# Graph attention over 8192 nodes on one core: the two dense inputs loaded as 128-row tiles, and row 0's store moved

## The reference

```python
h = jnp.maximum(_layernorm(x, axis=-1), 0.0)
g = inlayer2 @ W.T + b
f1 = g @ w1 + b1
f2 = g @ w2 + b2
logits = f1[:, None] + f2[None, :]
bias_mat = NEG_BIG * (1.0 - (adj > 0).astype(jnp.float32))
coefs = jax.nn.softmax(jax.nn.leaky_relu(logits, 0.01) + bias_mat, axis=-1)
out = x + coefs @ h
```

## Time and profile before

| What | Value |
|---|---|
| median of 3 runs | 1447.62 us (1447.36 to 1449.03) |
| the profiled execution's own time | 1447.61 us |
| its span, first to last instruction | 1445.8 us |
| PE busy | 1409.0 us (97%), 12623 matmuls |
| DVE busy | 1279.7 us (89%) |
| ACT busy | 612.7 us (42%) |
| POOL busy | 266.7 us (18%) |
| moved by DMA | 302.43 MB in 110184 packets |
| granted TensorE clock, mean | 0.990 |

### The profile page before, as it was taken

The page is one execution under the profiler, slowest core; times in us unless marked ns, Lnnn a source line. Parts: engine busy times, 40 slices in busy tenths (PEclk is TensorE's granted clock), DMA queues, the critical chain, the costliest instruction groups (busy, mean ns, idle before and its releaser), DMA issues.

```text
span 1445.8 us, 33385 instructions
## 1 busy us (share of the span) xinstructions
PE 1409.0 (97%) x12623; PEld 1246.9 (86%) x12623; DVE 1279.7 (89%) x1315; ACT 612.7 (42%) x713; POOL 266.7 (18%) x266
## 2 busy tenths in 40 slices
PE   8589899999999999999999999999999999999998
PEld 7468788888888888888888888888888888888887
DVE  5999898989989898998989899898998989899894
ACT  2895343444434344443434444343443434444330
POOL 0683111101101111110111111011111101111110
PEclk9799999999999999999999999999999999999999
DMA  9977999999999999999999999999999999999940
GB/s 293 316 177 167 228 233 235 234 235 221 209 210 215 209 210 210 214 210 208 216 207 211 211 213 211 208 216 206 213 213 211 210 209 215 209 209 216 208 108 14
DMA packets 110184, 302.43 MB, mean 209 GB/s; under 512 B 11732, under 2 KB 44628, under 8 KB 110164
## 3 DMA queue, kind: packets, MB, share of 16 engines
q1 hardware_dynamic: 100080, 289.52, 89.3%
q10 hardware_dynamic: 10084, 12.65, 3.0%
HBM read 293.73 MB, written 8.39 MB: 209 GB/s over the span
## 4 chain that ended last, share of the span: by engine, by line
PE 91%; DMA 4%; ACT 3%; issue 1%; DVE 1%; SPq 0%; ACTq 0%; POOL 0%; DVEq 0%; POOLq 0%
PE acc L1043 59%; PE acc L1045 29%; DMA adj_sb<-in_adj_dram 4%; PE rp L998 2%; ACT mask L561 1%; ACT h_f L577 1%; SPq L341 0%; ACT rp L561 0%; DMA w<-in_L_gnn_w_dram 0%; ACT H L583 0%; PE rp L1012 0%; PE small L985 0%; PE rp L1006 0%; DVE wgt L832 0%; ACTq L336 0%
## 5 line engine op out<-in xcount | busy, mean ns | idle before, releaser
L1043 PE MATMUL acc<-H,wT 128*128 128x257 f16 x8192 | 1356.7, 274 | 13.6 <-DVE wT L842 4.9
L1045 PE MATMUL acc<-H,wT 128*128 128x257 f16 x4096 | 1120.2, 273 | 0.0
L1043 PEld LDWEIGHTS acc<-H,wT 128*128 128x128 bf16 x8192 | 802.3, 98 | 116.4 <-issue 10.1
L561 ACT ACTIVATE mask<-adj_sb 128x1024 bf16<-128x1024 int32 x504 | 519.6, 1053 | 548.2 <-DVE wgt L832 432.8
L842 DVE STREAM_TRANSPOSE wT<-wgt 128x1024 f32<-128x1024 f32 x512 | 633.7, 1239 | 129.9 <-PE acc L1045 129.8
L832 DVE SCALAR_TENSOR_TENSOR wgt<-b_word,c_word,mask 128x1024 f32<-128x1024 f32 x504 | 628.7, 1260 | 3.6 <-ACT mask L561 3.6
L1045 PEld LDWEIGHTS acc<-H,wT 128*128 128x128 f16 x4096 | 401.9, 98 | 50.6
L481 POOL TENSOR_TENSOR x_res<-o_room,x_res 128x256 f32<-128x256 f32 x63 | 65.9, 1046 | 1100.6 <-ACT o_room L568 1077.4
L568 ACT ACTIVATE o_room<-acc,r_den 128x256 f32<-128x256 f32 x63 | 29.8, 474 | 230.6 <-DVE r_den L861 230.6
L486 POOL TENSOR_TENSOR o_room<-o_room,x_res 128x256 f32<-128x256 f32 x63 | 81.5, 1293 | 5.3
L483 POOL TENSOR_SCALAR o_room<-h_mean,no_nb 128x256 f32<-128x256 f32 x63 | 61.1, 969 | 0.0
(11 more groups left out here) (93 smaller groups left out, 163.4 us busy)
## 6 DMA issues: line engine op xcount, KB each, us to landing
adj_sb<-in_adj_dram SPq DMA_DIRECT2D x504, 512.0 KB, 8.5
x_res<-in_x_dram SPq DMA_DIRECT2D x64, 128.0 KB, 4.0
out_dram<-o_room SPq DMA_DIRECT2D x63, 128.0 KB, 4.3
H<-in_x_dram ACTq DMA_DIRECT2D x16, 256.0 KB, 12.7
H<-in_x_dram SPq DMA_DIRECT2D x16, 256.0 KB, 13.1
adj_sb<-in_adj_dram ACTq DMA_DIRECT2D x8, 512.0 KB, 14.3
wgt<-in_L_gnn_inlayer_dram ACTq DMA_DIRECT2D x8, 256.0 KB, 9.8
wgt<-in_L_gnn_inlayer_dram SPq DMA_DIRECT2D x8, 256.0 KB, 10.3
```

Of the source, the lines that this page charges most:

```text
L561: nc.scalar.activation(place, adj_sb[:, c, g * CQ:(g + 1) * CQ], ACT.Relu, scale=M_SCALE).then_inc(m_ready, 1)
L1043: pe.matmul(acc[:, par, 0:DV], w_hi[:, slot, t, :], H[:, j, part, 0:DV], start=(j == 0 and part == 0), stop=False)
L1045: mm = pe.matmul(acc[:, par, 0:DV], w_lo[:, slot, t, :], H[:, j, 0, 0:DV], start=False, stop=(j == ROWS - 1))
```

## The change

1. `load_strip` no longer loads a group of 32 partitions (8 rows of 1 KB for each) but a tile t of 128 rows over all partitions (1 KB each). A strip takes eight transfers of 128 KB in place of four of 256 KB, SP issues tiles 0 to 3 and ACT tiles 4 to 7. The bytes, the 1 KB pieces and the places where they land are the same. The waits for a strip count to 128 in place of 64. In memory the source of one transfer is four blocks, 1024 rows apart, of 32 adjacent rows; its outermost count is 4, where that of the destination is 128. Before, both outermost counts were 32.
2. SP stores row 0, and loads `x` for row 2, after it has issued the first chunk of row 4, not before (`store_row`, and one row more ahead of SP's loop).
3. Four small moves: ACT issues its half of row 1's first chunk before `values(2)`, not after its high half; ACT makes the first two mask parts of row 2 after the last high halves; DVE makes `weights(0, 0, 1)` ahead of `low_of_values(7)`; the mean of `h` is made one strip earlier on PE and two earlier on DVE.

```diff
-    x_q = x.rearrange("(c q k t s) d -> c k q s t d", c=NCH, q=Q, k=SC, t=TS)
-    in2_q = inlayer2.rearrange("(c q k t s) d -> c k q s t d", c=NCH, q=Q, k=SC, t=TS)
+    x_t = x.rearrange("(c q k t s) d -> c k t q s d", c=NCH, q=Q, k=SC, t=TS)
+    in2_t = inlayer2.rearrange("(c q k t s) d -> c k t q s d", c=NCH, q=Q, k=SC, t=TS)
...
-        def load_strip(eng, stage, source, k, signal, quadrants):
-            for q in quadrants:
-                eng.dma_start(stage[B * q:B * (q + 1), :, :], source[k // SC, k % SC, q]).then_inc(signal, 16)
+        def load_strip(eng, stage, source, k, signal, tiles):
+            for t in tiles:
+                eng.dma_start(stage[:, t, :], source[k // SC, k % SC, t]).then_inc(signal, 16)
...
-            first_loads(sp, (0, 1))
-            load_x(sp, 1, 4, (0, 1))
+            first_loads(sp, (0, 1, 2, 3))
+            load_x(sp, 1, 4, (0, 1, 2, 3))
...
+            def store_row(I, par, following):
+                sp.wait_ge(o_ready, I + 1)
+                sp.dma_start(out_rows[I], o_sb[:, par, :]).then_inc(o_stored[par], 16)
+                sp.dma_start(x_res[:, par, :], x_rows[following]).then_inc(x_loaded[par], 16)
...
-                    if n == NS - 1 and not (is_row(I, 0) or is_row(I, 1)):
-                        sp.wait_ge(o_ready, I - 1)
-                        sp.dma_start(out_rows[I - 2], o_sb[:, par, :]).then_inc(o_stored[par], 16)
-                        sp.dma_start(x_res[:, par, :], x_rows[I]).then_inc(x_loaded[par], 16)
-
-            row_tiles(sp, body, ahead=1)
+                    if n == NS - 1 and not (is_row(I, 0) or is_row(I, 1) or is_row(I, 2)):
+                        store_row(I - 2, par, I)
+                    if n == Q - 1 and is_row(I, 3):
+                        store_row(0, 0, 2)
+
+            row_tiles(sp, body, ahead=2)
...
-                act.wait_ge(xs_loaded[k], 64)
+                act.wait_ge(xs_loaded[k], 128)
...
             high_of_values(1)
+            second_adj(act, 0, (2, 3))
             values(2)
             high_of_values(2)
-            second_adj(act, 0, (2, 3))
...
-                dve.wait_ge(in2_loaded[k], 64)
+                dve.wait_ge(in2_loaded[k], 128)
...
-            low_of_values(7)
-            weights(0, 0, 1)
+            weights(0, 0, 1)
+            low_of_values(7)
...
```

More of the change, by code:

```diff
@@ L342, in load_adj, with load_in2, load_x, first_loads @@
                               adj_q[I, c, q]).then_inc(adj_loaded[c], 16)
-        def load_in2(eng, first, end, quadrants):
+        def load_in2(eng, first, end, tiles):
             for k in range(first, end):
-                load_strip(eng, in2_stage(k), in2_q, k, in2_loaded[k], quadrants)
-        def load_x(eng, first, end, quadrants):
+                load_strip(eng, in2_stage(k), in2_t, k, in2_loaded[k], tiles)
+        def load_x(eng, first, end, tiles):
             for k in range(first, end):
[L350 to L355, removed]
+                load_strip(eng, x_stage(k), x_t, k, xs_loaded[k], tiles)
+        def first_loads(eng, tiles):
+            load_in2(eng, 0, 4, tiles)
+            load_x(eng, 0, 1, tiles)
+            load_in2(eng, 4, 8, tiles)
         def first_adj(eng, c, quadrants):
@@ L369, in _ @@
             sp.dma_start(w12[:, 1:2], w2.rearrange("(h o) -> h o", o=1)).then_inc(w_loaded, 16)
[L370 to L371 removed]
+            first_loads(sp, (0, 1, 2, 3))
+            load_x(sp, 1, 4, (0, 1, 2, 3))
             first_adj(sp, 0, (0, 1))
[L373 removed]
+            load_x(sp, 4, 8, (0, 1, 2, 3))
             first_adj(sp, 1, (0, 1))
@@ L534, in _ @@
             act.dma_start(b12[:, 1:2], b2.rearrange("(h o) -> h o", o=1)).then_inc(biases_loaded, 16)
-            first_loads(act, (2, 3))
+            first_loads(act, (4, 5, 6, 7))
             def f_to_sbuf(c):
@@ L607, in _ @@
             sums(0)
-            load_x(act, 1, 2, (2, 3))
+            load_x(act, 1, 2, (4, 5, 6, 7))
             f_to_sbuf(0)
-            load_x(act, 2, 3, (2, 3))
+            load_x(act, 2, 3, (4, 5, 6, 7))
             squares(0)
-            load_x(act, 3, 4, (2, 3))
+            load_x(act, 3, 4, (4, 5, 6, 7))
             first_adj(act, 0, (2, 3))
-            load_x(act, 4, 5, (2, 3))
+            load_x(act, 4, 5, (4, 5, 6, 7))
             sums(1)
             f_to_sbuf(1)
-            load_x(act, 5, 6, (2, 3))
+            load_x(act, 5, 6, (4, 5, 6, 7))
             squares(1)
-            load_x(act, 6, 7, (2, 3))
+            load_x(act, 6, 7, (4, 5, 6, 7))
             act.wait_ge(f2_rel_ready, 1)
@@ L625, in _ @@
             b_of_chunk(1)
-            load_x(act, 7, 8, (2, 3))
+            load_x(act, 7, 8, (4, 5, 6, 7))
             values(0)
@@ L678, in _ @@
             high_of_values(14)
+            high_of_values(15)
+            mask_part(2, 0, 0)
+            mask_part(2, 1, 0)
             mask_part(2, 2, 0)
             mask_part(2, 3, 0)
-            high_of_values(15)
             scale_rows(0, 0, 0)
@@ L771, in raw_stats @@
                     if j == first or j % TS == 0:
-                        dve.wait_ge(xs_loaded[j // TS], 64)
+                        dve.wait_ge(xs_loaded[j // TS], 128)
                     nc.vector.bn_stats(out=pair_stats[:, j // 2, :],
@@ L961, in body @@
                                                 ALU.mult).then_inc(h_sum_ready, 1)
-                    if is_row(I, 2) and u == 5:
+                    if is_row(I, 2) and u == 3:
                         dve.wait_ge(h_mean_ps_ready, 1)
@@ L1097, in body @@
                     products(I, par, k)
-                    if is_row(I, 2) and k == 1:
+                    if is_row(I, 2) and k == 0:
                         pe.wait_ge(h_sum_ready, 1)
```

2 lines of the change are left out of this document (removed).

## The result

The changed kernel takes 1574.4 us (median of 4 runs, 1574.2 to 1575.2); the kernel before, on the same chip, 1448.3 (1447.4 to 1449.3). The ratio is 1.0867, 95% interval 1.0853 to 1.0881: 126 us slower. The prediction was 1584, between 1546 and 1612. The profiled execution took 1574.21 us, its span is 1572.4, 126.6 more than before.

The account below looks back on a forecast made before the run. PE was taken to bound 300 to 1400 us, so the change acts in the head, where the loads decide. 1447.6 + 141.6 (longer head) - 5.0 (store and small moves) = 1584.2 us, range 1546 to 1612.

Parts of the forecast that it names:

- Where the time is lost: Whole kernel: PE bounds 300 to 1400 us, untouched by the change; only the head changes, 141.6 us longer from the loads.
- Four engines: Strip loads: source outermost count 4 puts each new load on the same four DMA engines; chance 0.80, likeliest 1584 us.
- (a): Strip loads: all sixteen engines take part since 128 partitions are the destination; 1444.1 us, range 1441 to 1448; chance 0.11.
- (c): Strip loads: eight engines, sixteen strips take 96.4 us, 48.2 more; 1488 us; chance 0.06 for eight or another number.
- (b): Strip loads: sixteen engines, but a queue holding a fixed number of transfers, so half the bytes; 1450 us; chance 0.03.
- The rate of an engine: Strip loads: each of four engines keeps 21.8 GB/s; a strip takes 12.06 us, sixteen 192.9, 144.6 us more.
- a fifth faster, as an allowance: Strip loads, lower bound: four engines might each be faster; 154 us for the strips, 38.6 less, 1546 us.
- The `adj` chunks between the strips: Head: `adj` transfers keep their shape, queue behind the strips and land later with them, by the whole 144.6 us.
- What ACT pays for issuing: Head: 64 issues in place of 32; ACT's last 28 take 15 us but vanish in the blocked queue: 0.
- Store and mean: End of head: moving row 0's store removes PE's 3.96 us wait, 4.0 us less; the mean of `h` gives 0.
- The 1.0 for the small moves: Head: `weights(0, 0, 1)` fills DVE's 1.31 us wait, so DVE's work for PE comes earlier; 1 us less.
- What would show it: Head signs: rate near 87 GB/s, share 0.27, ACT computing near 95, groups 12 us apart, PE starting 140 us later.

Follow-up runs that it names:

- e3: The changed kernel with eight 128 KB transfers a strip, each over 32 partitions, outermost count 32 on both sides: 1442.9 us, ratio 0.9965.
- e5: The changed kernel with each tile of 128 rows read from 8 separate blocks of 16 adjacent rows: 1491.1 us, ratio 1.029.
- e8: The changed kernel with each tile of 128 rows read from 2 separate blocks of 64 adjacent rows: 1755.9 us, ratio 1.212.
- e4: The changed kernel with each tile of 128 rows read from 128 adjacent rows, outermost count 128 on both sides: 1443.4 us, ratio 0.997.
- e1: The changed kernel with the loads of both inputs as before, four 256 KB transfers a strip over 32 partitions each: 1441.8 us, ratio 0.9958.
- e10: The kernel before with only row 0's store moved behind row 4's first chunk and SP one row more ahead: 1442.8 us, ratio 0.9961.
- e12: The kernel before with three small moves (ACT's earlier issue, ACT's mask order, DVE's earlier weights), without the mean of `h`: 1447.9 us, ratio 0.9995.
- e2: The kernel before with the new loads alone; store and small moves as before: 1584.1 us, ratio 1.0933.
- run 140: Not a follow-up kernel: words of the forecast that PE's unbroken run of work starts some 140 us later; measured 132.2.

## Why the prediction was right, and where it was not

**Where the time is lost: right.** PE is bound from 300 us on, nothing there changed (212 against 210 GB/s, PE full); all of it is in the head.

**Four engines: right.** 4 small packets a load, a share of 0.27, and the series 2, 4, 8, 16. Rivals (a) and (c) fell by the packets and the share, (b) by these and by e3.

**The rate of an engine: right in mechanism, mis-sized.** This is the term of the sum that was off most. It took 348/16 = 21.8 GB/s and 12.06 us a strip. An engine did 24.1 and a strip took 10.89, so sixteen strips cost 174.2 in place of 192.9, and 126.0 us more than before instead of 144.6. The prediction had allowed this ("a fifth faster, as an allowance") in the range only, and worked it out as a fifth off the time, which is an engine a quarter faster; 24.1 is a tenth faster. e5 and e8 show 24.0 as well, e4 with sixteen 21.9. What slows each of sixteen no run shows.

**The `adj` chunks between the strips: missing in the sum.** They were taken as moving with the strips. The trace's landing times say otherwise. The `x` strips around row 0's first chunk land at 125.7, 143.6 and 159.5, which is 12.0 us more than two strips' pace; the last lands at 199.9, 7.8 over its own. Before, the same shortfalls are some 9 us together, so this gives back 10.8 of the 18.6. The bytes don't explain it: a sixteenth of a chunk is 131 KB, 5.4 us of an engine at 24.1 GB/s, and 6.0 before at 21.8. What changed is the rate beside a chunk. Between 130 and 138 us a packet of 1 KB takes 84 to 113 ns in place of 46, and all sixteen engines together move 182 GB/s from 131 to 140 at a share of 0.87. Before, such a packet went from 51 ns to 59 to 71 beside the same chunk. The slowing goes with the tile over 128 partitions and not with four engines: e4 has it with all sixteen (79 to 89 ns, 16.8 us of shortfalls), e1 and e3 with their 32 partitions have 8.5 and 8.2. It is part of e5's 9 us too (95 to 108 ns beside the chunk). Why wide tiles and `adj` transfers slow each other is open.

The last strip thus lands at 199.9 and not 65.5, 134.4 later: 126.0 + 10.8, less 2.4 that the start and smaller differences gave (the prediction took 3). ACT's masks, which the prediction made the measure of the head, came 132.2 later against the forecast 141.6, because the chunk behind the last strip landed 12.8 us after it (212.7), where before it was 15.0 (80.5). The head came out 9.4 under its forecast because the rate's error of 18.6 and this missing term have opposite signs; that part of the closeness is luck.

**What ACT pays for issuing: right.** 0 with four engines; all its issues are inside the blocked queue. ACT came out of its last issues at 180.1, 20 us before the last strip landed, within the 12 to 24 of the forecast. With sixteen engines e3 has as many issues and is 1.1 us over e1, where rival (a) had 1 to 2; the runs of the two touch, so the size isn't told.

**Store and mean: right wait, wrong owner, wrong price.** The wait is gone and in e10 the chunks landed within 3 us of what was worked out. But "the mean of `h` moves within work that nobody waits for: 0" was wrong: POOL waits for it (137.76, behind `h_mean`), SP waits for POOL, row 4's chunk stands behind SP. It costed the first half of that chain at the store and did not ask why the store was late. In the sum it did no harm, since both edits remove one wait. The price of the wait was 4.0 and is 5.6, since the clock behind it was left out. The 1.0 for the small moves isn't seen: DVE's `turn` for row 1 is 131.0 us later (219.21 against 88.20), 1.2 less than the masks, but PE's long run begins the full 132.2 later, and e12 gains nothing clear of noise. So 5.0 was forecast and 5.6 measured in these traces, by two errors that cancel. Against e2 the same edits are worth 9.7 us, and 4 of these are unexplained.

**The sum.** 1447.6 + 132.2 (PE's long run begins later) - 4.0 (the wait) - 1.6 (the clock behind it) = 1574.2. Of the 10 us between forecast and result 9.4 are the head. By runs with and without them, the new loads cost 132.6 us beside the other edits (against e1) and 135.5 on their own (e2 against the kernel before), where 141.6 was forecast.

**What would show it.** 87 GB/s forecast, 96 measured; 0.27 and 0.27; ACT's first work near 95, 92.8; groups 12 us apart, 10.9; PE's run 140 us later, 132.2. One sign did not come: no wait of ACT for `H` from `x` shows. Its idle time ahead of these statistics, 46.3 us in three pieces, is put down to its own issues.

## What to carry to other kernels

Here a transfer whose source had an outermost count of 2, 4 or 8 ran on that many DMA engines only: count the small packets of a queue, or read the busy share, before a tile is made "wider". Put the loop with the large count outermost on both sides, even if the transfer then fills fewer partitions. And where a store is late, ask what its producer waits for; two edits that free the same wait are worth it once. Read the granted clock behind a wait of PE as well; here it made a wait of 4 us cost 5.6.

## What the runs showed that was not expected

- A DMA engine with 1 KB pieces moves 24.0 to 24.1 GB/s when 2, 4 or 8 are at work, and 21.9 when all 16 are (350 GB/s).
- Two kernels with sixteen engines each and the same pieces differ, 128 adjacent source rows against 16 blocks: 342 and 267 GB/s from 4 to 9 us, 1443.4 and 1455.0 us in all.
- With 32 partitions a transfer, two queues reach 344 to 348 GB/s (e3 and the kernel before), with 128 partitions 350 (e4): no gain from the wider tile once the queues are full, and a loss while an `adj` chunk lands (269 against 328 GB/s from 34 to 46 us). From 4 to 9 us the rates are 219 with 256 KB transfers, 290 with 128 KB over 32 partitions (e3) and 342 over 128 (e4), but e4 as a whole is no faster than e1.
- PE had the lower of its two clock levels, 1.2 GHz (0.50 granted), from 120 to 140 us, a stretch in which it had nothing to do. It costs nothing there, since the loads set the pace. From 171.0 to 174.4 us of the kernel before it costs 1.6 us.
- The kernel before with the earlier mean of `h` alone, two numbers in the source, is some 6 us (0.4%, interval 0.26 to 0.54%) faster than the kernel before, and no kernel here is faster than it by more than the spread.
